# First mixture of a decoder kernel: sorted rows and 71 tiles in place of all eight experts per token

## The reference, cut to what matters

```
def _swiglu(h):
    x_glu = jnp.minimum(h[..., ::2], 7.0)
    x_lin = jnp.clip(h[..., 1::2], -7.0, 7.0)
    return x_glu * sigmoid(1.702 * x_glu) * (x_lin + 1.0)
t = (x * rsqrt(mean(x * x) + 1e-5) * norm_scale)        # 4096 tokens x 128
top_v, top_i = top_k(t @ gate_w + gate_b, 2)            # of 8 experts
w = zeros(T, 8) with softmax(top_v) at top_i
y = sum over e of w[:, e] * (_swiglu(t @ w1[e] + b1[e]) @ w2[e] + b2[e])   # w1: 128x512, w2: 256x128
x = _layernorm(x + (x + y))
```

## Time and profile before

| | us |
|---|---|
| median of three runs | 4215.26 |
| runs | 4212.34 to 4217.67 |
| span of the profiled execution, its first to its last instruction | 4213.5 |
| PE busy | 3630.4 (86%) |
| DVE busy | 2669.3 (63%) |
| ACT busy | 2153.0 (51%) |
| POOL busy | 1214.6 (29%) |

### The profile page before, as it was taken

One profiled execution on the slowest core, in us unless ns is written; L12 is line 12 of the kernel. 1 busy time (PEld: TensorE's weight loads), 2 busy tenths in 40 slices (PEclk: granted clock), 3 DMA queues, 4 the chain that ended last, 5 costly groups with the idle time before them and its releaser, 6 DMA issues. The chain is left out here.

```text
span 4213.5 us, 80834 instructions
## 1 busy us (share of the span) xinstructions
PE 3630.4 (86%) x31554; PEld 2445.2 (58%) x31554; DVE 2669.3 (63%) x7122; ACT 2153.0 (51%) x3863; POOL 1214.6 (29%) x798
## 2 busy tenths in 40 slices
PE   2999998788999789989999996554689999798999
PEld 2777776565666655655555553343357776565665
DVE  6788887566888778666566555885532222796555
ACT  2677776444555456455555545441654444475232
POOL 3555453222223144015445552321200000252000
PEclk8999999998999889999999997776889999898999
DMA  4333332000000010000000000004200000000000
GB/s 125 53 55 57 53 55 37 4 1 1 1 1 1 1 56 2 1 1 2 2 2 2 2 2 1 22 22 119 86 7 1 1 1 1 31 2 1 1 11 11
DMA packets 59734, 87.71 MB, mean 21 GB/s; under 512 B 16746, under 2 KB 43708, under 8 KB 58364
## 3 DMA queue, kind: packets, MB, share of 16 engines
q1 hardware_dynamic: 58922, 82.40, 8.4%
q10 hardware_dynamic: 434, 0.15, 0.0%
HBM read 40.43 MB, written 8.52 MB: 12 GB/s over the span
## 5 line engine op out<-in xcount | busy, mean ns | idle before, releaser
L856 PE MATMUL banks<-XT,weight_region 128*128 128x512 f32 x1696 | 782.0, 600 | 1.4 <-DVE T L1231 1.4
L878 PEld LDWEIGHTS banks<-weight_region,HT 128*128 128x128 f32 x4672 | 561.4, 192 | 128.6 <-issue 107.4
L878 PE MATMUL banks<-weight_region,HT 128*128 128x128 f32 x4672 | 566.6, 275 | 6.4 <-ACT HT L1013 5.9
L1254 DVE SCALAR_TENSOR_TENSOR x_res<-banks,WT,x_res 128x128 f32<-128x128 f32 x800 | 225.2, 344 | 476.5 <-PE banks L878 437.2
L856 PEld LDWEIGHTS banks<-XT,weight_region 128*128 128x128 f32 x1696 | 305.9, 193 | 288.1 <-issue 285.3
L1008 ACT ACTIVATE HT<-banks,weight_region 128x512 f32<-128x512 f32 x256 | 173.3, 687 | 239.4 <-PE banks L856 233.2
L1071 POOL TENSOR_TENSOR FNM<-FNM,FRS 128x8 f32<-128x8 f32 x16 | 3.2, 202 | 965.5 <-ACT FRS L967 965.5
L458 DVE TENSOR_REDUCE MX<-banks 128x8 f32<-128x1152 f32 x128 | 173.2, 1353 | 102.0 <-PE banks L275 101.9
L1727 POOL TENSOR_TENSOR SM<-SM,RZ 128x1232 f32<-128x1232 f32 x64 | 143.8, 2247 | 188.5 <-DVE RZ L1769 187.3
L1024 ACT ACTIVATE T<-banks 128x512 f32<-128x512 f32 x128 | 76.1, 597 | 234.1 <-PE banks L856 226.2
L384 ACT COPY PT<-banks 128x384 f32<-128x384 f32 x384 | 170.4, 478 | 47.0 <-PE banks L285 43.3
(11 more groups left out here) (487 smaller groups left out, 8315.3 us busy)
## 6 DMA issues: line engine op xcount, KB each, us to landing
FL<-RAW SPq DMA_DIRECT2D x512, 64.0 KB, 2.3
weight_region<-in_l_ffn__w_dram SPq DMA_DIRECT2D x4, 2048.0 KB, 7.8
T<-s4d_k_dram SPq DMA_DIRECT2D x8, 1024.0 KB, 9.3
film_dram<-F SPq DMA_DIRECT2D x8, 512.0 KB, 2.9
FO<-film_dram SPq DMA_DIRECT2D x8, 512.0 KB, 4.0
x_res<-in_x_dram SPq DMA_DIRECT2D x1, 2048.0 KB
weight_region<-in_l_ffn__w_dram SPq DMA_DIRECT2D x2, 1024.0 KB, 9.9
s4d_u_dram<-U SPq DMA_DIRECT2D x8, 256.0 KB, 2.0
```

What stands on the lines that cost most here:

```text
L856: nc.tensor.matmul(PS[:, q % 4, :], w, xt, start=True, stop=True).then_inc(s.h_ps, 1)
L878: ins = nc.tensor.matmul(PS[:, 4 + u % 2, b * P:(b + 1) * P], HT[:, u % 2, j, b * P:(b + 1) * P], w2[j], start=j == 0, stop=j == len(w2) - 1)
L1254: ins = nc.vector.scalar_tensor_tensor(R[:, t, :], PS[:, 4 + u % 2, b * P:(b + 1) * P], WT[:, t, e:e + 1], R[:, t, :], ALU.mult, ALU.add)
```

## The change

l0_ffn becomes routed(..., kind "swiglu"), with KTOP = 2 and NT = 71 tiles (2 x 32 + 7). Its steps are:

1. The same norm, transposes and logits for all four pairs, and pick (the two best experts of each token, SEL). ranks(gp): nine bf16 products count, for each token and expert, the tokens ahead of it that chose the same expert. slots(gp): expert number x 4096 plus that count is a row number in a DRAM tensor sorted_rows of 33792 rows; each token gets two (IDX). table(): from the counts, which expert (EJI) and which first row (ROWI) each of the 71 tiles has. A tile past an expert's last token is filled up with whatever stands in those rows; zeros are written there first.
2. move(gp), on GpSimd: per block and choice one indirect transfer writes 128 rows of TN to their row numbers, 64 in all.
3. 71 tiles. SP: fetch(j) reads the register ROWI and loads 128 rows; put(j) writes the result over the same rows. GpSimd: stage(j) reads EJI and copies that expert's weights (128x772) and output bias (128x128) to one of three buffers. TensorE: turn_rows, up, down. ScalarE: columns, bend (Silu). VectorE: clip, gate, rows_out.
4. bring(g), on GpSimd: 64 indirect transfers read the results back to token order (G); combine(g) adds them with the weights WK to 2x, and the layer norm follows.

The 33 writes of zeros to sorted_rows, 512 KB each, stand in the prefetch lists of the four passes of l0_xattn. The weights are laid out anew so that an expert's lie together (wall). Nothing of the other sublayers is changed.

```diff
--- before.py
+++ after.py
@@ -1327,7 +1327,564 @@
...
+ROWS = B_ALL * P
+ZROWS = 8 * P
+SORTED = 8 * ROWS + 8 * P
...
+def routed(nc, E, kind, rows, b2=None, prefetch=(), store=None):
...
+    NT = KTOP * NB + NE - 1
...
+    LD, ST = 4, 4
+    LEAD = 3
...
+                def ranks(gp):
+                    pe.wait_ge(s.sel, gp + 1)
+                    if gp == 0:
+                        pe.wait_ge(s.zero, 1)
+                    if gp >= 2:
+                        pe.wait_ge(s.total, gp - 1)
+                    o = place_bank(gp).rearrange("p t e -> p (t e)")
+                    m = SEL[:, gp % 2].rearrange("p t e -> p (t e)")
+                    nc.tensor.matmul(o, BEF[:], m, start=True, stop=False)
+                    for d in range(1, PB + 1):
+                        n = min(PB, PB + 1 - d)
+                        ins = nc.tensor.matmul(o[:, d * NE:(d + n) * NE], ONE[:], m[:, 0:n * NE], start=False, stop=d == PB)
+                    ins.then_inc(s.pre_ps, 1)
...
+                def turn_rows(j):
+                    pe.wait_ge(loads[j % LD], 16 * (j // LD + 1))
+                    if j >= 2:
+                        pe.wait_ge(s.xs, j - 1)
+                    nc.tensor.transpose(turned(j), XR[:, j % LD, :], E.ident).then_inc(s.t_ps, 1)
+
+                def up(j):
+                    pe.wait_ge(s.xs, j + 1)
+                    pe.wait_ge(s.staged, j + 1)
+                    if j >= 2:
+                        pe.wait_ge(s.hid, j - 1)
+                    w = WR[:, j % 3, 0:UP]
+                    for c in range(4):
+                        at = (c + 2) % 4 if kind == "gated" else c
+                        ins = nc.tensor.matmul(up_bank(j, c // 2)[:, (c % 2) * P:(c % 2 + 1) * P], w[:, at * P:(at + 1) * P], XC[:, j % 2, :], start=True, stop=True)
+                        if c % 2 == 1:
+                            ins.then_inc(s.h_ps, 1)
+
+                def down(j):
+                    pe.wait_ge(s.hid, j + 1)
+                    if j >= 2:
+                        pe.wait_ge(s.y_sb, j - 1)
+                    w = WR[:, j % 3, UP:UP + hb * P]
+                    for c in range(hb):
+                        ins = nc.tensor.matmul(down_bank(j), HT[:, j % 2, c, :], w[:, c * P:(c + 1) * P], start=c == 0, stop=c == hb - 1)
+                    ins.then_inc(s.y_ps, 1)
...
+                pe.wait_ge(s.total, NPAIR)
+                for j in range(NT + 2):
+                    if j < NT:
+                        turn_rows(j)
+                    if 1 <= j <= NT:
+                        up(j - 1)
+                    if j >= 2:
+                        down(j - 2)
...
+                def fetch(j):
+                    if j >= LD:
+                        sp.wait_ge(s.t_ps, j - LD + 1)
+                    r = nc.sync.value_load(ROWI[0:1, j:j + 1], min_val=0, max_val=SORTED - P)
+                    sp.dma_start(XR[:, j % LD, :], rows[bass.ds(r, P), :]).then_inc(loads[j % LD], 16)
+
+                def put(j):
+                    r = nc.sync.value_load(ROWI[0:1, j:j + 1], min_val=0, max_val=SORTED - P)
+                    sp.wait_ge(s.y_sb, j + 1)
+                    sp.dma_start(rows[bass.ds(r, P), :], Y[:, j % ST, :]).then_inc(stores[j % ST], 16)
+
+                sp.wait_ge(s.tab, 1)
+                sp.wait_ge(E.moved, 16 * KTOP * NB)
+                for j in range(NT + LEAD):
+                    if j < NT:
+                        fetch(j)
+                    if j >= LEAD:
+                        put(j - LEAD)
...
+                def columns(j):
+                    act.wait_ge(s.t_ps, j + 1)
+                    if j >= 2:
+                        act.wait_ge(s.h_ps, 2 * (j - 1))
+                    if rms:
+                        nc.scalar.activation(XC[:, j % 2, :], turned(j), ACT.Identity, scale=W.scale).then_inc(s.xs, 1)
...
+                def move(gp):
+                    pool.wait_ge(s.cast, gp + 1)
+                    if rms:
+                        pool.wait_ge(s.tn, 2 * gp + 2)
+                    for i in range(PB):
+                        t = gp * PB + i
+                        for k in range(KTOP):
+                            nc.gpsimd.indirect_dma_start(out=rows, out_offset=bass.IndirectOffsetOnAxis(ap=IDX[:, k, t:t + 1], axis=0),
+                                                         in_=(TN if rms else E.x)[:, t, :], in_offset=None,
+                                                         bounds_check=SORTED - 1, oob_is_err=False).then_inc(E.moved, 16)
...
+                def stage(j):
+                    e = nc.gpsimd.value_load(EJI[0:1, j:j + 1], min_val=0, max_val=NE - 1)
+                    if j >= 3:
+                        pool.wait_ge(s.y_ps, j - 2)
+                    if has_b2:
+                        if j >= 3:
+                            pool.wait_ge(s.y_sb, j - 2)
+                        nc.gpsimd.tensor_copy(B2S[:, j % 3, :], B2R[:].rearrange("p e d -> p (e d)")[:, bass.ds(e * P, P)]).then_inc(s.b2, 1)
+                    nc.gpsimd.tensor_copy(WR[:, j % 3, :], W.wall.rearrange("p e n -> p (e n)")[:, bass.ds(e * STAGED, STAGED)]).then_inc(s.staged, 1)
...
+                def bring(g):
+                    for b in range(GB):
+                        t = g * GB + b
+                        for k in range(KTOP):
+                            nc.gpsimd.indirect_dma_start(out=G[:, k, t, :], out_offset=None, in_=rows,
+                                                         in_offset=bass.IndirectOffsetOnAxis(ap=IDX[:, k, t:t + 1], axis=0),
+                                                         bounds_check=SORTED - 1, oob_is_err=False).then_inc(gathers[g], 16)
+
+                for gp in range(NPAIR):
+                    move(gp)
+                pool.wait_ge(s.tab, 1)
+                if has_b2:
+                    pool.wait_ge(s.b2_ld, 16)
+                for j in range(NT):
+                    stage(j)
+                for o in range(ST):
+                    pool.wait_ge(stores[o], 16 * len(range(o, NT, ST)))
...
+                def clip(j):
+                    b1 = WR[:, j % 3, 6 * P:6 * P + 4]
+                    if j >= 2:
+                        dve.wait_ge(s.h_act, j - 1)
+                        dve.wait_ge(s.hid, j - 1)
+                    dve.wait_ge(s.h_ps, 2 * j + 1)
+                    for c in range(2):
+                        ins = nc.vector.tensor_scalar(T1[:, j % 2, c, :], up_bank(j, 0)[:, c * P:(c + 1) * P], b1[:, c:c + 1], 7.0, ALU.add, ALU.min)
+                    ins.then_inc(s.h_clip, 1)
+                    dve.wait_ge(s.h_ps, 2 * j + 2)
+                    for c in range(2):
+                        ins = nc.vector.tensor_scalar(T3[:, j % 2, c, :], up_bank(j, 1)[:, c * P:(c + 1) * P], b1[:, 2 + c:3 + c], 8.0, ALU.add, ALU.min)
...
+                        nc.vector.scalar_tensor_tensor(HT[:, j % 2], T3[:, j % 2], -6.0, T2[:, j % 2], ALU.max, ALU.mult).then_inc(s.hid, 1)
...
+                def rows_out(j):
+                    dve.wait_ge(s.y_ps, j + 1)
+                    if j >= ST:
+                        dve.wait_ge(stores[j % ST], 16 * (j // ST))
+                    if has_b2:
+                        dve.wait_ge(s.b2, j + 1)
+                        nc.vector.scalar_tensor_tensor(Y[:, j % ST, :], down_bank(j), 1.0 / SLOPE if kind == "swiglu" else 1.0, B2S[:, j % 3, :],
+                                                       ALU.mult, ALU.add).then_inc(s.y_sb, 1)
...
+                def combine(g):
+                    dve.wait_ge(gathers[g], 16 * GB * KTOP)
+                    if rms:
+                        dve.wait_ge(s.two, g // 2 + 1)
...
+                for gp in range(NPAIR):
+                    if rms and gp + 1 < NPAIR:
+                        rms_stats(gp + 1)
+                    pick(gp)
+                    slots(gp)
+                table()
+                for j in range(NT + 1):
+                    if j < NT and kind == "swiglu":
+                        clip(j)
+                    if j >= 1:
+                        rows_out(j - 1)
+                    if j < NT and kind != "gelu":
+                        gate(j)
+                for g in range(NG + 1):
+                    if g < NG:
+                        combine(g)
+                        final_stats(g)
+                    if g >= 1:
+                        final_apply(g - 1)
...
-def l0_ffn(nc, E, **kw): moe(nc, E, "swiglu", **kw)
...
+def l0_ffn(nc, E, **kw): routed(nc, E, "swiglu", **kw)
...
+        sorted_rows = scratch_dram("sorted_rows", [SORTED, P])
...
+        block_of = lambda a, n: a[n * ZROWS:(n + 1) * ZROWS].rearrange("(p q) d -> p (q d)", q=8)
+        clean = [(block_of(sorted_rows, n), block_of(dram["zeros"], 0)) for n in range(SORTED // ZROWS)]
         nothing = lambda i: {}
-        chunks("a", ("l0_xattn", l0_xattn, lambda i: {"prefetch": l1_cross if i == 0 else ()}))
-        run("l0_ffn", l0_ffn)
```

(7 more changed lines are left out.)

362 lines of the change are left out of this document (added).

## The result

The changed kernel takes **4277.31 us** (median of four runs, 4275.36 to 4278.74) against 4215.98 us of the kernel before in the same measurement: 1.0144 times as long, 95% interval 1.0129 to 1.0158. It is 61.3 us slower where 42.5 were forecast. The time lies inside the range of 4155 to 4365 us, and the side, slower, is the one that had the most chance.

A forecast was written before the change was run, and what follows sets the result against it. The prediction took TensorE's matmul work to bound the stage. Routing, scatters, 71 tiles, gathers and the last combine ended it at 1437.6 against 1395.1 us, 42.5 longer: from 4215 to 4258 us, range 4155 to 4365.

The forecast's parts named there:

- What bounds the stage: The changed stage: TensorE, busy 300.00 of 300 us, bounds it; its work falls about 234 us, nearly all replacement work is serial.
- Part 1: Routing to the first scatter: logits, pick, 1.2 us of ranks and 1.8 of row numbers, first index at 1034.0 us.
- The other three pairs go on beside the scatters, hidden: Routing of later pairs: 43 us of VectorE, hidden while 16 scatters last longer than one pair's 11 us.
- Part 3: The tile loop: SP's order allows two tiles per round trip, 3.1 us a tile, 220.1 us for 71.
- Rival (c): The tile loop runs at VectorE's pace, 2.0 us a tile, through short landing and register load: 4180 us; chance 0.11.
- Part 4: The way back: 64 gathers at 1.3 us, combining beside them except the last group's, stage end at 1437.6 us.
- What costs nothing: Clearing the sorted rows in l0_xattn is hidden in SP's waits, three small constants in the first load likewise.
- the reserve of 4 us: Clearing in l0_xattn: at twice the load price, nine transfers take 72 us and the first pass would give 4 us.
- Rival (d): In the tiles, VectorE's gate product and GpSimd's weight copy contend for a shared port, 0.4 us: 4286 us; chance 0.07.

The follow-up runs named there:

- f1: Changed kernel with each of the 128 indirect transfers moving 64 of its 128 rows, half the tokens' results left out: 4252.87 us, ratio 1.0084.
- e7: Changed kernel with eight row buffers, six tiles of lead, one row-number read, delayed fill, earlier first rank products, two gather pauses: 4192.21 us, 0.9944.
- e2: Changed kernel with the first scatter waiting until the row numbers of all four pairs are there: 4303.86 us, ratio 1.0203.
- e1: Changed kernel with eight row buffers for four and put six tiles behind fetch for three: 4229.45 us, ratio 1.0027.
- e3: Changed kernel with each group of eight gathers waiting until the group ahead has landed: 4273.77 us, ratio 1.0132.
- e4: Kernel before with only the 33 writes of zeros added in the cross-attention's four passes: 4216.02 us, ratio 0.9995.
- e8: Changed kernel with a wait for landing in the middle of each pair's 16 scatters: 4269.90 us, ratio 1.0127.
- f3: e7 with a wait for landing in the middle of the first three pairs of scatters: 4187.47 us, ratio 0.9930.

## Why the prediction was right, and where its sum was off

The stage by the prediction's own terms (us; measured from the rows above):

| term | forecast | measured | difference |
|---|---|---|---|
| start of the stage | 1016.6 | 1023.12 | +6.5 |
| to the first scatter | 17.4 | 20.7 | +3.3 |
| 64 scatters | 83.2 | 90.7 | +7.5 |
| landing, 71 tiles, last store | 229.5 | 212.4 | -17.1 |
| 64 gathers | 83.2 | 83.1 | -0.1 |
| from the last gather to the end | 7.7 | 20.9 | +13.2 |
| end of the stage | 1437.6 | 1451.1 | +13.5 |
| the rest of the kernel, against before | 0 | +7.5 | +7.5 |

The spans differ by 63.5 us = 42.5 + 13.5 + 7.5.

- **What bounds the stage** was right: less matmul work, and 174 us (90.7 + 83.1) in which GpSimd makes 128 transfers and TensorE has little or nothing, 12.8 us in the scatters and none in the gathers. Chance was spread by the price of one transfer, and it came out at 1.27 and 1.30 us against 1.3. It was right on weak legs: the working took it by the row (three steps for each of 128), and f1 shows that it is by the transfer (0.07 us for 64 rows). That a mechanism of the wrong kind gave the right 1.3 is luck.
- **Part 1** missed 3.3 us. It put the rank products behind the choice of the first pair and nothing else; in TensorE's list the transposes and logits of the second pair stand between, and VectorE waited 3.6 us for them where 1.2 were forecast. The other 1.0 us lies between the row numbers (1042.86) and the first transfer (1043.83), for which the sum had nothing. The table of the order ahead of the prediction had it. e7 moves them and gets 3.0 back.
- **"The other three pairs go on beside the scatters, hidden"** named its condition, that a pair takes less than 16 scatters. Undisturbed it does (in e2 the first row numbers stood at 1044.1 and the last let the first scatter go at 1081.3, 12.4 us a pair, against 16 x 1.27 = 20). Held by the scatters it took 25, and GpSimd waited 4.74 and 4.82 us. No row of before could show this, since it had no such transfers; the step took an engine's time beside another engine for the same as alone.
- **Part 3** was right in mechanism, SyncE's round trip with two tiles in it, and e1 shows it. The size was 0.25 us too long per tile, 2.85 for 3.1, from two terms. The TENSOR_LOAD takes 0.27 us where 0.6 was taken. And 3.1 was chosen between 5.7/2 at the full clock and 6.9/2 at the lower one; the granted clock was forecast below 0.9 in the tiles and was 0.93 in the third stretch above. At the full clock and with 0.27 the forecast's sum gives (5.7 - 0.33)/2 = 2.7. The Trainium skill (DMA: Bandwidth & Descriptors, Latency and other measured facts) gives a floor of about 600 ns for tensor_load; the trace, with a median of 269 ns, decides against it here. Rival (c) was said to be impossible with two landings in four tiles. That holds for the change as written; with eight buffers and one load fewer, the loop does run at 1.82.
- **Part 4** costed combining at nothing but for the last group. That step failed, for the same hold: 13.2 us, the largest miss of the sum. e3 and e7 show the same combining without it, with 7.3 us to the end where 7.7 were forecast.
- **"What costs nothing"**: the clearing was hidden, in e4 and in the changed kernel; the reserve of 4 us was not needed. What did cost was not looked for: one cast at the start of the first attention, 3.5 us there and about 4 in all.
- **The rest of the kernel** gave 7.5 us more, in sublayers that the change does not touch. Between their barriers they took 2815 to 2817 us in three executions of the kernel before and its variants and 2818 to 2828 in ten of the changed ones. It is not one place: the mixing sublayer of the second layer took 380.1 to 382.5 us in the former and 384.8 to 388.1 in the latter, while the second layer's cross-attention, with 210.9 to 211.5 against 208.5 to 213.6, shows nothing. The cause stays open; placement of data and weights is only a guess.
- **Rival (d)** is half right: a hold beside GpSimd exists and costs, but in the tiles, where it was put, HT took 0.43 us, its plain price. The Trainium skill (SBUF — State Buffer, Who interferes with whom) says of a cast in a two-port mode that whoever issues first gets the shared pair and the other fully blocks. The cast of 3.89 us ends with a fill of 3.54 beside it, which agrees in kind but not in the order: the cast had begun 0.27 us ahead of the fill, and in the kernel before the same two did not block each other. The section also says that "PE and ACT never wait on anyone". As to ports nothing here speaks against that: the products stand at their time (1055.83), and what comes 10.5 us late is the rise of their semaphore.
- **The sum as a whole** came out nearer than its terms: 38.0 us of terms set too low (start, first scatter, scatters, last gather to end, rest) stand against 17.2 set too high, most of them in the tiles. That they cancel in part is luck.

## What to carry to other kernels

Before work is traded for indirection, count the transfers, not the rows: at 1.3 us each, GpSimd alone sets 128 x 1.3 us here, and a transfer of 64 rows costs nearly what one of 128 does. A loop that waits for a register load, a DMA out and a DMA in needs its depth from the whole round trip, and when it has that, the issuing engine's own instructions are next: eight buffers and one register load fewer were worth 78 us. Work that is "hidden beside GpSimd's transfers" must be looked at in a trace, at the rises of semaphores too; in the gathers a break of 2 us every 24 gathers kept VectorE at full pace.

## What the runs showed of the hardware

- An indirect transfer of GpSimd takes 0.97 us (scatter) or 1.00 us (gather) for 128 rows of 512 bytes, 0.90 and 0.94 for 64, and 0.30 us to the next.
- In a long unbroken row of gathers of 128 rows the semaphores of VectorE rise up to 8.8 us after their instructions have ended, and instructions that wait for them start whole multiples of 0.70 us apart; in the scatters TensorE's rise up to 10.5 us late (11.5 in e8). Rises are missing from the trace in the same stretches. In the gathers the first late rise came after 28 to 35 transfers in all six kernels with 128 rows and no breaks, and the last within 7 us of the last transfer's start; with breaks after every 8 or 24, or with 64 rows per transfer, it didn't occur. In the scatters the first came after 7 to 10 transfers, in e8 after 17; with 64 rows it didn't occur, and with a break in the middle of a pair's 16 it did in e8 and didn't in f3. The mechanism is open, and whether it is there without the profiler no run tells.
- A cast of 128x128 on VectorE took 3.89 us beside a fill by GpSimd, and 0.42 beside the same fill in the kernel before.
- SyncE's TENSOR_LOAD of one number takes 0.27 us, and the instructions that come with it 0.17.
